# A two-layer convolution kernel on one core: x in partition order, 2048-byte scratch lines, x1 written first, tiles 1 and 2 in one buffer, grouped work split at 16

## What is computed

```python
def ref_L0(xn):                      # xn = group norm of x, 32 groups of 16 channels
    f = relu(Wc @ xn + bc)           # 512 -> 128 channels
    gk = relu(mean(xn) @ Wc.T + bc)[..., None] * Wkk + bkk
    sk = relu(Wc @ max_3x3_blocks(xn) + bc)
    dynW = relu(Wck @ stack(gk, sk) + bck)   # 128 kernels of 3x3 per output, of each image its own
    y = conv3x3(f, dynW) + b_ad
    return Wf @ y + bf               # 128 -> 512 channels
x1 = x + ref_L0(_gn(x))
out = x1 + conv3x3_grouped(_gn(x1), kernels)   # 32 groups of 16 channels
```

## Time and profile before

| | |
|---|---|
| median of 3 runs | 4184.36 us (4183.64 to 4201.24) |
| the profiled execution | 4183.85 us, its span 4182.1 us |
| mean granted TensorE clock | 0.947 of full |
| busy: PE, DVE, ACT, POOL | 3557.2, 2980.8, 2180.7, 981.9 us |
| moved | 810.21 MB, mean 194 GB/s |
| SP's queue, ACT's queue | 68.0% and 9.7% of the 16 engines' span |

### The profile page before, as it was taken

One profiled execution on the slowest core, in us unless ns is written; L12 is line 12 of the kernel. 1 busy time (PEld: TensorE's weight loads), 2 busy tenths in 40 slices (PEclk: granted clock), 3 DMA queues, 4 the chain that ended last, 5 costly groups with the idle time before them and its releaser, 6 DMA issues.

```text
span 4182.1 us, 64976 instructions
## 1 busy us (share of the span) xinstructions
PE 3557.2 (85%) x18048; PEld 2746.5 (66%) x18048; DVE 2980.8 (71%) x8020; ACT 2180.7 (52%) x3911; POOL 981.9 (23%) x1036
## 2 busy tenths in 40 slices
PE   5688988889888889888898888898888988888886
PEld 4566766667666667666676666676666766666764
DVE  7776776768676767776777767677777777676752
ACT  4364554555444655555655446554456554465444
POOL 2121221222212212212212122122122121222223
PEclk9899999999999999999999999999999999999998
DMA  6878777887778787779777788877797777878746
GB/s 105 203 206 204 192 171 202 220 209 198 174 190 218 204 211 198 175 191 225 198 211 177 182 212 207 207 199 172 187 227 202 206 181 183 211 209 211 197 98 174
DMA packets 389593, 810.21 MB, mean 194 GB/s; under 512 B 67250, under 2 KB 297012, under 8 KB 376756
## 3 DMA queue, kind: packets, MB, share of 16 engines
q1 hardware_dynamic: 375220, 658.76, 68.0%
q10 hardware_dynamic: 14336, 151.00, 9.7%
HBM read 501.40 MB, written 308.28 MB: 194 GB/s over the span
## 4 chain that ended last, share of the span: by engine, by line
issue 66%; POOL 20%; PE 5%; DMA 4%; DVE 3%; SPq 1%; POOLq 1%; ACT 0%; ACTq 0%; DVEq 0%
POOL hl L405 20%; DMA tb<-x_rows 1%; DMA x_rows<-x1b 1%; PE pd L905 1%; POOLq L404 1%; PE pb L905 1%; PE pb L907 1%; PE pd L906 1%; PE pb L906 1%; PE pd L907 1%; DVE bst L631 1%; SPq L324 1%; DVE mx L633 1%; DMA tb<-x 1%; DMA out<-tb 0%
## 5 line engine op out<-in xcount | busy, mean ns | idle before, releaser
L405 POOL TENSOR_TENSOR hl<-un,hl 128x384 f16<-128x384 f32 x1024 | 954.3, 932 | 3120.2 <-ACT hl L430 3119.9
L905 PE MATMUL pd<-hl,k_h 128*96 128x384 f16 x3072 | 1051.2, 342 | 466.0 <-POOL hl L405 389.1
L906 PE MATMUL pd<-hl,k_h 128*96 128x384 f16 x3072 | 1045.0, 340 | 0.0
L907 PE MATMUL pd<-hl,k_l 128*96 128x384 f16 x3072 | 1042.1, 339 | 0.0
L816 DVE SCALAR_TENSOR_TENSOR tb<-pd,kout,tb 96x384 f32<-96x384 f32 x1024 | 622.9, 608 | 433.9 <-PE pd L907 427.4
L426 ACT ACTIVATE un<-tb,b_t,s_t 128x384 f32<-128x384 f32 x1024 | 710.7, 694 | 389.8 <-DMA tb<-x_rows 388.2
L905 PEld LDWEIGHTS pd<-hl,k_h 128*96 128x96 f16 x3072 | 392.1, 128 | 653.9 <-issue 353.9
L430 ACT ACTIVATE hl<-un 128x384 f16<-128x384 f32 x1024 | 538.8, 526 | 301.8 <-PE pd L907 269.0
L805 DVE SCALAR_TENSOR_TENSOR x1b<-pac,bfc,xb 128x288 f32<-128x288 f32 (+2 forms) x1408 | 543.3, 429 | 85.0 <-PE pac L907 79.9
L905 PE MATMUL pb<-fh,dynh 128*128 128x480 f32 (+1 forms) x1440 | 554.2, 385 | 8.2 <-DVE dynl L710 8.2
L907 PE MATMUL pb<-fh,dynl 128*128 128x480 f32 (+1 forms) x1440 | 549.6, 382 | 0.0
(11 more groups left out here) (107 smaller groups left out, 4163.7 us busy)
## 6 DMA issues: line engine op xcount, KB each, us to landing
x_rows<-x1b SPq DMA_DIRECT2D x128, 1152.0 KB, 16.2
tb<-x_rows SPq DMA_DIRECT2D x128, 1152.0 KB, 12.1
out<-tb ACTq DMA_DIRECT2D x128, 1152.0 KB, 8.1
tb<-x SPq DMA_DIRECT2D x372, 384.0 KB, 10.7
xb<-x SPq DMA_DIRECT2D x124, 720.0 KB, 9.8
xb<-x SPq DMA_DIRECT2D x124, 432.0 KB, 16.6
tb<-x_rows SPq DMA_DIRECT2D x256, 192.0 KB, 13.5
x_rows<-mrow SPq DMA_DIRECT2D x64, 96.0 KB, 17.7
```

The costliest lines, as they stand in the source:

```text
L405: pool.tensor_tensor(hl[:, g % HL_RING, 1, :, 1:W + 1], un[:, g % U_RING], hl[:, g % HL_RING, 0, :, 1:W + 1], ALU.subtract).then_inc(hl_lo, 1)
L905: pe.matmul(acc, high_w, high_x, start=start, stop=False)
L906: pe.matmul(acc, high_w, low_x, start=False, stop=False)
L907: return pe.matmul(acc, low_w, high_x, start=False, stop=stop)
```

## The change

x is handed in with its channels reordered, so that a quarter's 128 rows lie in the order of the partitions. A line of the scratch tensor has 2048 bytes for 1920, with x1 256 bytes into it. SP writes x1 as soon as it is complete, then loads the second part of x, then writes the means. Tile 0 has a slot of its own, tiles 1 and 2 share one. The split is at 16; ACT stores tile 0 behind group 12 as before, and tile 1 behind `dynh`.

```diff
-ROW = BW + 2 * W
+ROW = 512
+AT = 64
-D_FIRST = 13
+D_FIRST = 16
-AT_SQUARES = (18, 20, 23, 26)
-AT_X1_VARIANCES = 27
+AT_SQUARES = (20, 22, 25, 27)
+AT_X1_VARIANCES = 28
-PREP_AT = (5, 6, 7, 8, 9, 11)
+PREP_AT = (5, 6, 8, 9, 11, 13)
-STORE_AT = {20: 1, 28: 2}
-TAIL_STORE_AT = {12: 0, 20: 1}
+STORE_AT = {28: 2}
+TAIL_STORE_AT = {12: 0, 15: 1}
-T_SLOT = [0, 1, 0, 2]
+T_SLOT = [0, 1, 1, 2]
-    x_d = x.rearrange("n (q j c) h w -> n q c j (h w)", q=Q, c=GC)
+    x_d = x.rearrange("n (q p) h w -> n q p (h w)", q=Q)
...
             def write_x1(n):
                 sp.wait_ge(x1_done, (n + 1) * X1_OPS)
+                src = x1b[:, :, :, :, :].rearrange("p q k b w -> p q k (b w)")
+                for c in range(Q):
+                    sp.dma_start(sc_w[n, c, :, :, AT:AT + BW], src[:, c]).then_inc(x1_out, 16)
+
+            def write_means(n):
                 sp.wait_ge(mrow_done, n + 1)
-                src = x1b[:, :, :, :, :].rearrange("p q k b w -> p q k (b w)")
-                sp.dma_start(sc_m[n, 0, :, :, W + BW:], mrow[:, :, :]).then_inc(x1_out, 16)
-                sp.dma_start(sc_m[n, OR_ - 1, :, :, 0:W], mrow[:, :, :]).then_inc(x1_out, 16)
-                for c in range(Q):
-                    sp.dma_start(sc_w[n, c, :, :, W:W + BW], src[:, c]).then_inc(x1_out, 16)
+                sp.dma_start(sc_m[n, 0, :, :, AT + BW:AT + BW + W], mrow[:, :, :]).then_inc(x1_out, 16)
+                sp.dma_start(sc_m[n, OR_ - 1, :, :, AT - W:AT], mrow[:, :, :]).then_inc(x1_out, 16)
...
-                reached(sp, stored[{0: 2, 2: 0}.get(c, c)], (n + 1 if c == 2 else n) * 16)
+                reached(sp, stored[{1: 2, 2: 1}.get(c, c)], (n + 1 if c == 2 else n) * 16)
...
                     load_t(n - 1, 3)
+                write_x1(n)
                 if more:
                     load_x(n + 1, 1)
-                write_x1(n)
+                write_means(n)
...
             def step(n, d=True, more=True, last=True):
                 a_phase(n, d, last)
                 if d:
-                    d_groups(n - 1, range(EARLY, D_FIRST))
+                    d_groups(n - 1, range(EARLY, D_FIRST - 3))
                     store(n - 1, 0)
+                    d_groups(n - 1, range(D_FIRST - 3, D_FIRST))
                 act.wait_ge(dyn_sum, 2 * (n + 1))
                 act.activation(dynh[:, :, :], dtmp[:, :, :], ACT.Relu).then_inc(dyn_hi, 1)
+                if d:
+                    store(n - 1, 1)
```

More of the change, by code:

```diff
@@ L306, in load_x @@
                 for c in range(Q):
-                    sp.dma_start(xb[:, c, lo:hi], x_d[n, c, :, :, lo:hi]).then_inc(x_in[part], 16)
+                    sp.dma_start(xb[:, c, lo:hi], x_d[n, c, :, lo:hi]).then_inc(x_in[part], 16)
             def stage_x(n, pieces):
@@ L313, in stage_x @@
                     sp.wait_ge(prep_done, PIECES * n + i - STAGES + 1 if i >= STAGES else PIECES * n)
-                    sp.dma_start(x_stage[:, i % STAGES, :], x_d[n, c, :, :, band * BAND:(band + 1) * BAND]).then_inc(staged[i % STAGES], 16)
+                    sp.dma_start(x_stage[:, i % STAGES, :], x_d[n, c, :, band * BAND:(band + 1) * BAND]).then_inc(staged[i % STAGES], 16)
             def write_x1(n):
                 sp.wait_ge(x1_done, (n + 1) * X1_OPS)
+                src = x1b[:, :, :, :, :].rearrange("p q k b w -> p q k (b w)")
+                for c in range(Q):
+                    sp.dma_start(sc_w[n, c, :, :, AT:AT + BW], src[:, c]).then_inc(x1_out, 16)
+            def write_means(n):
                 sp.wait_ge(mrow_done, n + 1)
-                src = x1b[:, :, :, :, :].rearrange("p q k b w -> p q k (b w)")
-                sp.dma_start(sc_m[n, 0, :, :, W + BW:], mrow[:, :, :]).then_inc(x1_out, 16)
-                sp.dma_start(sc_m[n, OR_ - 1, :, :, 0:W], mrow[:, :, :]).then_inc(x1_out, 16)
-                for c in range(Q):
-                    sp.dma_start(sc_w[n, c, :, :, W:W + BW], src[:, c]).then_inc(x1_out, 16)
+                sp.dma_start(sc_m[n, 0, :, :, AT + BW:AT + BW + W], mrow[:, :, :]).then_inc(x1_out, 16)
+                sp.dma_start(sc_m[n, OR_ - 1, :, :, AT - W:AT], mrow[:, :, :]).then_inc(x1_out, 16)
             def load_t(n, c):
@@ L329, in load_t @@
                     sp.wait_ge(x1_out, (n + 1) * X1_DMAS)
-                reached(sp, stored[{0: 2, 2: 0}.get(c, c)], (n + 1 if c == 2 else n) * 16)
+                reached(sp, stored[{1: 2, 2: 1}.get(c, c)], (n + 1 if c == 2 else n) * 16)
                 above, below = partition_of(0), partition_of(IR - 1)
                 dst = t_slot(c).rearrange("p j b w -> p j (b w)")
-                sp.dma_start(dst[0:M6], sc_k[n, c, :, :, W:W + BW]).then_inc(t_in[c], 16)
-                sp.dma_start(dst[above:above + GC], sc_k[n, c, M6 - GC:M6, :, 0:BW]).then_inc(t_in[c], 16)
-                sp.dma_start(dst[below:below + GC], sc_k[n, c, 0:GC, :, 2 * W:]).then_inc(t_in[c], 16)
+                sp.dma_start(dst[0:M6], sc_k[n, c, :, :, AT:AT + BW]).then_inc(t_in[c], 16)
+                sp.dma_start(dst[above:above + GC], sc_k[n, c, M6 - GC:M6, :, AT - W:AT - W + BW]).then_inc(t_in[c], 16)
+                sp.dma_start(dst[below:below + GC], sc_k[n, c, 0:GC, :, AT + W:AT + W + BW]).then_inc(t_in[c], 16)
             def step(n, d=True, more=True):
@@ L1031 @@
     laid_out = {
-        "x": np.asarray(x),
+        "x": np.asarray(x).reshape(N, Q, GQ, GC, H, W).transpose(0, 1, 3, 2, 4, 5).reshape(N, C, H, W),
         "wct": np.asarray(L0_conv_Wc).reshape(CM, Q, GQ, GC).transpose(3, 2, 1, 0).reshape(P, Q, CM),
```

## The result

The changed kernel takes **4276.25 us** (median of 4 runs, 4272.51 to 4279.77); the kernel before took 4188.4 us beside it (4 runs, 4183.64 to 4201.24). The ratio is 1.0205, 95% interval 1.0178 to 1.0231. So the kernel became slower, clear of noise; whether by more or less than 2% the interval leaves open. The forecast was 4200 us. The range, 4030 to 4340, held the result, and the sum was 76 us short.

What follows compares the result with a forecast made beforehand. It took waits, not a busy engine, to bound the kernel, chiefly ACT's for tile transfers. 31 x (-10.8 + 5.8) = -155, 30 times S3 +165 and ends +6 made +16 on 4183.85: 4200 us, range 4030 to 4340.

Steps and rivals of the forecast that it cites:

- x in partition order: x loads ahead of tile 0's load: 393 GB/s as plain rows, 7.8 us less in S1.
- S1: PE's stretch from the first grouped matmul behind B to group 0: 61.2 us becomes 50.4, set by transfers.
- One store fewer in S1: Tile 1 is stored ahead of B, so its 1.18 MB leave S1: 3.0 us less.
- x1 first, means last: Order of SP's transfers ahead of tile 0's load: nothing gained, since that load waits for all of them.
- The cover that was worked out for A's fourth tile: In the A phase: the later x part 1 still lands about 4 us before the fourth tile reads it.
- Scratch lines: Scratch tensor lines of 2048 bytes for 1920: same bytes moved, 0 in the sum.
- S2: PE's stretch of groups from group 0 up to B: 24.6 us becomes 30.4, +5.8 per image.
- the half piece of statistics: In S2, two operations move from before group 10 to group 13, out of a DVE-bound stretch: -1.0 us.
- S3: PE's stretch B: late tile 2 load delays piece 6, gap grows, half clock follows; 41.9 us becomes 47.4, +5.5.
- Ends: First and last image: first x quarter -3, x1 before means -2, tile 2's last wait 11 later; +6 us.
- rival 1: Aligned lines are worth something or B's new wait is smaller: about 4030 us, 4115 with half; chance 0.27.
- rival 2: x loads no faster, HBM read sets their rate, so the 7.8 us stay in S1: 4442 us; chance 0.10.
- rival 3: Line pitch slows x1's write to 290 GB/s, or half clock through more of B: 4280 us; chance 0.17.

Runs made afterwards that it cites:

- x_order: Kernel before with only x put in partition order and read by plain rows; 3924.78 us, ratio 0.9375.
- buffers_back: Changed kernel with tiles 0 and 2 sharing a buffer again and tile 1 stored behind group 20; 4046.95 us, ratio 0.9654.
- late-store kernels: split_store_late, and the changed kernel with the two mends and tile 3's store behind A's fourth tile of converts; 3755.48 and 3769.92 us.
- x_first: Kernel before with x in partition order and x1 written first, means last, lines still 1920 bytes; 3902.53 us, ratio 0.9328.
- split_back: Kernel before with x in partition order, 2048-byte lines and x1 written first; 3915.15 us, ratio 0.9331.
- high_early: Changed kernel with ACT making the kernels' high part ahead of the converts of groups 13 to 15; 4145.29 us, ratio 0.9906.
- piece6: Changed kernel with SP issuing piece 6 of x ahead of tile 2's load; 4020.49 us, ratio 0.9623.
- the two mends: The edits of high_early and piece6; both together on the changed kernel measured 3927.48 us, ratio 0.9387.
- split_store_late: split_back with piece 6 issued ahead of tile 2's load and tile 3's store behind A's fourth tile of converts; 3755.48 us, ratio 0.8986.

## Why the prediction was right or wrong

Taken by its steps:

- *x in partition order*, -7.8 us in S1: right in kind, 0.8 small. x_order measured 8.64; I had taken 393 GB/s, x alone ran at 419.
- *One store fewer in S1*, -3.0: mis-sized. It is worth 1.15 us (buffers_back against the changed kernel): the load of tile 0 is issued 2.0 us sooner (34.9 to 32.9 us behind B's end), and group 0 follows it 0.9 us later (17.1 to 18.0). The same happens over the whole change. Every byte saved let the load of tile 0 leave earlier, but tile 3's store moved by 5.8 us only (37.4 to 31.6 us behind B's end) and came to stand right ahead of that load. Issue to group 0 grew from 13.99 to 17.95 us, and took back 4.0 of the 15.2 us by which the issue had moved (48.11 to 32.92 us behind B's end). The late-store kernels show it. I had priced the line by its bytes and not looked at who would meet whom at its end.
- *S1* in sum: -11.3 for -10.8. By the chain x_order, x_first, split_back, buffers_back, changed kernel: x -8.64, order -0.51, lines +0.72, split -1.73, the store -1.15. So the sum was nearly right with terms that were not: that is luck. PE's idle time ahead of group 24 went as forecast (2.26 us before, 0.13 after, at the mean), and 3.8 us of that at group 0 stayed, for the 5.6 forecast.
- *x1 first, means last*, nothing: right within 0.5% with 1920-byte lines, wrong with 2048, where it is worth 1.7% on x in order. The cover that was worked out for A's fourth tile held: the A phase takes 15.73 us in both kernels.
- *Scratch lines*, 0: right in the company of x1 first (0.9328 and 0.9331), wrong alone (0.984).
- *S2*, +5.8: measured +8.2. The three groups and the 2.4 us wait were right (2.25 in the image shown). Two terms failed. The -1.0 for the half piece of statistics was worth nothing: the stretch was not DVE-bound where it was taken out. Output 7 to 8 was 1.45 us with it, and is 1.09 without (2140.84 to 2141.93); but then DVE stands 0.49 us for PE, which needs 1.48 a group, and output 10 ends a steady image's groups as late as before (it starts 19.04 us behind output 0; 19.02 before). And the gap at group 13 has a price behind it: half clock in 17 of the 26 images; groups 13 and 14 took 1.80 and 2.24 us from start to start at the mean for 1.48, 1.1 together. The half clock at group 0 also cost 0.3 more. I had priced the clock behind B's gap and not behind this one; high_early shows the gap and its price together, 3.77 us.
- *S3*, +5.5: measured +6.45. Tile 2 left 6.80 us into B for 6.7. PE's idle time grew by 4.4 at the mean (1.5 to 5.9) for 4.1, and the rest of the growth, 2.0, is the half clock behind it, for 1.4. The cause was right (piece6), but I had given it to the buffers as a fixed cost, and it is one place in SP's queue: buffers_back and piece6 both end at 39.37.
- *Ends*, +6: tile 2's wait in the last image is 22.37 us for 11.27, the 11 forecast. The 3 us booked for the first quarter of x gained nothing: the first A phase starts at 40.8 us in both kernels. The wait for tile 0 in the last image fell by 6.3 (20.97 to 14.65), more than the 2 booked; x1 first is most of it (21.13 in x_order, 15.66 in x_first).

The miss of 76 us: 31 x 2.4 in S2 and 30 x 0.95 in S3 are 103, less 31 x 0.5 in S1, about 87; the other -11 are not traced further than the ends above. Rival 1 got the lines right and the sum wrong, since with x1 first nothing of them was left; rival 2 fell; rival 3 came within 4 us of the result with 4280, by luck: the write of x1 did not get slower (it lands in 12.1 us for 16.2), and the half clock in B added 0.6 us per image to what was booked, where the rival needed over 2. The upper end of the range is said to be half of rival 2's way; that is 4321 and not 4340, which changes nothing here. That the change as a whole loses is now shown in parts: x, order and lines together are worth -6.7% (split_back); the split takes 3.2% and the buffers 5.5% (buffers_back and the changed kernel), 8.7% together, of which the two mends give back 8.2 without touching either.

## What to carry to other kernels

A load that waits for a semaphore holds all that stands behind it in its queue: before a buffer is shared anew, look which later transfers need nothing of that wait and put them ahead. Where transfers are the bound and are made fewer, ask what now stands directly ahead of the one that releases the engines; a store that nobody waits for belongs behind it. And price a gap on TensorE with the half clock that follows it, while a piece of work taken from an engine counts only up to the pace of the next one.

## What the runs showed of the hardware

- The same x bytes moved at 228 to 238 GB/s in a 16 by 8 row pattern and at 386 to 419 as plain rows in partition order. The Trainium skill (DMA: Bandwidth & Descriptors, "The descriptor swizzle") gives each engine one SBUF port in a plain 128-partition transfer. That the 16 by 8 pattern breaks this is an inference. The rates agree with it, but the order in which x is read from HBM changed with the pattern, and the ports no run here shows.
- A load of 1.57 MB was followed by the first matmul that needs it in 14.0 us with a store of 1.18 MB issued 10.7 us ahead of it (before), in 18.0 us with the store 1.3 ahead (changed), and in 13.8 with the store behind it (split_store_late).
- PE's granted clock fell to 0.50 behind an idle time of 1.5 us in B in 4 of 26 images (before). In the changed kernel it fell behind 2.25 us at group 13 in 17 of 26, behind 3.8 us at group 0 in 25 and behind 5.9 us in B in all.
- The place of a store on ACT's queue moved PE's A phase by 0.6 us: it takes 15.73 us with the store issued behind the first tile of converts and 15.13 with it behind the fourth. Whether the issue itself or its transfer costs this is not shown.
- Lines that start on 256 bytes gave 1.6% in one arrangement of the same transfers, nothing in another and cost 1.3% in a third. The cause stays open.
